# Moving the energies up in TensorE's order and joining four scan products with one wide GpSimd addition

## What is computed

```python
x = whitening(x)         # quaternion batch norm: covariance of 4 channel groups, Cholesky, mix, bias
x = mamba(x)             # layer norm, W_in, causal conv of 4 taps, silu, then the scan:
    def step(hst, xs):
        d_t, B_t, C_t, u_t = xs
        dA = jnp.exp(d_t[:, :, None] * A)
        hst = hst * dA + (d_t * u_t)[:, :, None] * B_t[:, None, :]
        y_t = jnp.einsum('bdn,bn->bd', hst, C_t)      # sum over 16 states
    y = (ys + xc * Dp) * silu(z);  out = W_out y + x
x = self_attention(x)    # softmax(q^T k) over 1024 x 1024 points, gamma * v attention + x
x = nonlocal_block(x)    # softmax of theta^T phi over 1024 x 1024 points, conv, batch norm over all images, + x
```

## Time and profile before

| | |
|---|---|
| median of three runs | 5754.26 us (5746.75 to 5754.81) |
| the profiled execution's own time | 5758.38 us |
| its span | 5756.6 us |
| TensorE, matmul | 4756.3 us busy, 83% |
| VectorE | 5060.5 us busy, 88% |
| ScalarE | 3713.5 us busy, 65% |
| GpSimd | 4706.1 us busy, 82% |
| mean granted TensorE clock | 0.929 of 2.4 GHz |

### The profile page before, as it was taken

One profiled execution on the slowest core, in us unless ns is written; L12 is line 12 of the kernel. 1 busy time (PEld: TensorE's weight loads), 2 busy tenths in 40 slices (PEclk: granted clock), 3 DMA queues, 4 the chain that ended last, 5 costly groups with the idle time before them and its releaser, 6 DMA issues.

```text
span 5756.6 us, 61917 instructions
## 1 busy us (share of the span) xinstructions
PE 4756.3 (83%) x17331; PEld 2758.9 (48%) x17331; DVE 5060.5 (88%) x5978; ACT 3713.5 (65%) x6077; POOL 4706.1 (82%) x3342
## 2 busy tenths in 40 slices
PE   6568888888888888888888888888888888888771
PEld 6134554555445445545554454455455544544451
DVE  4689999999999999999999999999999999999933
ACT  3456666667666666666676667666766766666633
POOL 0698988888888888888888988888888889888910
PEclk9679999999999999999999999999999999999995
DMA  4456555555565555656655655655566566555527
GB/s 130 182 219 223 221 201 218 220 220 211 217 220 211 209 221 216 218 208 220 220 204 219 223 215 211 218 216 204 219 220 220 208 219 225 212 207 219 214 82 295
DMA packets 199099, 1216.87 MB, mean 211 GB/s; under 512 B 27880, under 2 KB 28656, under 8 KB 67696
## 3 DMA queue, kind: packets, MB, share of 16 engines
q1 hardware_dynamic: 194416, 1196.26, 56.6%
q10 hardware_dynamic: 4352, 16.78, 0.7%
HBM read 1158.43 MB, written 54.53 MB: 211 GB/s over the span
## 4 chain that ended last, share of the span: by engine, by line
PE 34%; DVE 29%; issue 14%; ACT 12%; POOL 8%; DMA 1%; DVEq 1%; SPq 0%; POOLq 0%; ACTq 0%
DVE hs L488 12%; PE psE L814 12%; DVE psD L484 11%; PE psA L814 10%; PE psT L814 6%; POOL pa L300 5%; DVE nm L513 3%; PE psT L987 3%; ACT da L680 3%; ACT p L726 3%; PE psY L814 2%; DVE psU L477 1%; POOL pa L306 1%; ACT L649 1%; ACT L751 1%
## 5 line engine op out<-in xcount | busy, mean ns | idle before, releaser
L300 POOL TENSOR_TENSOR pa<-hs,rows_all 128x1024 f32<-128x1024 f32 x1024 | 2411.3, 2355 | 522.7 <-DVE hs L488 522.2
L680 ACT ACTIVATE da<-delta,neg_a 128x512 f32<-128x512 f32 x2048 | 1375.7, 715 | 224.9 <-DVE hs L488 212.6
L484 DVE TENSOR_TENSOR psD<-rows_all,psU 128x512 f32<-128x512 f32 x2048 | 1415.9, 691 | 84.6 <-POOL hlast L304 6.0
L488 DVE TENSOR_TENSOR_SCAN hs<-da,hlast,psD 128x512 f32<-128x512 f32 x1024 | 1310.8, 1280 | 36.3
L306 POOL TENSOR_TENSOR pa<-pa 128x512 f32<-128x512 f32 x1024 | 1301.2, 1271 | 40.1
L488 DVE TENSOR_TENSOR_SCAN hs<-da,psD 128x512 f32<-128x512 f32 x1024 | 1249.2, 1220 | 35.2
L726 ACT ACTIVATE p<-psE,nm 128x1024 f32<-128x1024 f32 x512 | 569.6, 1113 | 633.8 <-DVE nm L513 633.8
L814 PE MATMUL psA<-pt,va 128*128 128x256 f32 x4096 | 954.2, 381 | 1.0 <-DVE x L531 0.6
L814 PEld LDWEIGHTS psA<-pt,va 128*128 128x128 f32 x4096 | 772.5, 192 | 194.9 <-issue 105.9
L513 DVE TENSOR_REDUCE nm<-psE 128x1 f32<-128x1024 f32 x512 | 618.6, 1208 | 275.5 <-PE psE L814 272.3
L690 ACT ACTIVATE pt<-psT 128x512 f32<-128x512 f32 x1024 | 554.9, 591 | 342.5 <-PE psT L987 332.8
(11 more groups left out here) (186 smaller groups left out, 5087.6 us busy)
## 6 DMA issues: line engine op xcount, KB each, us to landing
rows_all<-bc_scratch SPq DMA_DIRECT2D x1024, 1024.0 KB, 4.7
xin<-x SPq DMA_DIRECT2D x40, 512.0 KB, 7.8
xres<-x SPq DMA_DIRECT2D x64, 256.0 KB, 6.3
x_scratch<-x SPq DMA_DIRECT2D x32, 512.0 KB, 4.2
f_scratch<-fa SPq DMA_DIRECT2D x32, 512.0 KB, 6.8
xres<-x SPq DMA_DIRECT2D x8, 512.0 KB, 3.7
x1g<-x SPq DMA_DIRECT2D x8, 512.0 KB, 3.6
fa<-x SPq DMA_DIRECT2D x8, 512.0 KB, 3.7
```

The lines of the kernel that those rows point to most:

```text
L300: pool.tensor_tensor(pa[:, k % PROD, :, :], hs[:, sl, :, :], rows_all[:, slot, 2:4, :], ALU.mult).then_inc(S["prod"], 1)
L484: dve.tensor_tensor(psD[:, :], rows_all[:, slot, j, :], psU[:, :], ALU.mult).then_inc(S["dbu_ok"], 1)
L488: dve.tensor_tensor_scan(hs[:, sl, j, :], da[:, sl, j, :], psD[:, :], hlast[:, h, n_:n_ + 1] if ch else 0.0, ALU.mult, ALU.add).then_inc(S ...
L680: act.activation(da[:, k % 2, j, :], delta[:, h, cols(ch)], ACT.Exp, scale=neg_a[:, h, 2 * q + j:2 * q + j + 1]).then_inc(S["da_ok"], 1)
```

## The change

Two parts. In GpSimd's `products`, the addition of the two states of a pair in every step goes. In odd steps one addition of 1024 columns adds the two pairs as they stand, and one of 512 columns adds the two halves of the result; the semaphore `pair` counts half as many. In TensorE's order the word `energy` moves in some rows, a new word `energy_next` issues the energy of the tile that belongs to the next step, and `add`, `skip0` and `weigh0` move with them.

```diff
@@ -302,12 +302,12 @@
-                    wait(pool, "prod", b, k + 1)
-                    pool.tensor_tensor(pa[:, k % PROD, 0, :], pa[:, k % PROD, 0, :], pa[:, k % PROD, 1, :], ALU.add
-                                       ).then_inc(S["pair"], 1)
                     if k % 2:
-                        wait(pool, "pair", b, k + 1)
-                        pool.tensor_tensor(pa[:, k % PROD, 0, :], pa[:, (k - 1) % PROD, 0, :], pa[:, k % PROD, 0, :], ALU.add
+                        wait(pool, "prod", b, k + 1)
+                        pool.tensor_tensor(pa[:, k % PROD, :, :], pa[:, (k - 1) % PROD, :, :], pa[:, k % PROD, :, :], ALU.add
+                                           ).then_inc(S["pair"], 1)
+                        wait(pool, "pair", b, (k + 1) // 2)
+                        pool.tensor_tensor(pa[:, k % PROD, 0, :], pa[:, k % PROD, 0, :], pa[:, k % PROD, 1, :], ALU.add
                                            ).then_inc(S["quad"], 1)
@@ -1034,22 +1034,22 @@
-                    "centre energy add variance",
-                    "energy turn add weigh0",
+                    "centre add variance",
+                    "add energy turn weigh0",
...
-                    "steps energy add weigh0",
...
+                    "add energy steps weigh0",
...
@@ -1100,6 +1100,8 @@
+                                        if what == "energy_next" and o + 1 in TILE_STEP:
+                                            energy(a, *TILE_STEP[o + 1], scan)
```

More of the change, by code:

```diff
@@ L180, in build @@
             u_ok=2 * NCH, dbu_ok=2 * STEPS, da_ok=2 * STEPS, h_ok=2 * STEPS,
-            hlast_ok=STEPS // 2, prod=STEPS, pair=STEPS, quad=STEPS // 2, quad_mm=STEPS // 2, g_ok=2 * NCH,
+            hlast_ok=STEPS // 2, prod=STEPS, pair=STEPS // 2, quad=STEPS // 2, quad_mm=STEPS // 2, g_ok=2 * NCH,
             x1_mm=NCH, x1_ok=NCH, x1g_ok=NCH,
@@ L1044, in _ @@
                     "energy add",
-                    "energy turn add skip0",
-                    "gates add",
-                    "energy rows turn add",
-                    "steps energy add weigh0",
[L1049 to L1052, removed]
+                    "skip0 energy turn add",
+                    "gates add energy_next",
+                    "rows turn add",
+                    "add energy steps weigh0",
+                    "turn weigh1 turn_more skip1 add energy_next",
+                    "add",
+                    "weigh0 energy turn add",
+                    "turn weigh1 add energy_next",
                 ]
```

## The result

The changed kernel takes 5704.15 us (median of 6 runs, 5701.91 to 5705.79), the kernel before 5754.37 us on the same chip. The ratio is 0.9917, with a 95% interval from 0.9905 to 0.993: 50 us or 0.8% faster. The forecast was 5715 us. In the runs further down, one execution of `tile3_tile4` (6114.69 us) and one of the kernel before (5962.21 us) fell in a slower state of the chip and are left out.

The account below looks back on a forecast made before the run. VectorE's waits, mostly for the energy of tile 3, were taken to bound the kernel. Per image 3.8 - 2.5 - 0.1 = 1.2 us, times 31 = 37 us off 5754, gave a forecast of 5715 us, range 5645 to 5825.

Parts of the forecast that it names:

- What bounds the kernel: VectorE leads at 93% busy inside images; its row maxima wait 6.4 us per image, 5.2 of them at tile 3.
- Energy of tile 3 ahead of `steps`: At tile 3 in both halves, VectorE's waits of 2.48 and 2.70 us shrink to 0.7 each: gain 3.8 us per image.
- the moved `add` fills some of TensorE's idle time: Ahead of tile 3's energy, the add fills some idle time but not most, so 0.7 us of wait stays per half.
- Tile 4 "counted as hidden": At r = 13 tile 4's late energy adds some 1 us of wait, counted as hidden there because GpSimd's chain starts later.
- GpSimd's additions by themselves: In GpSimd's products, 0.19 us less work per pair of steps; nothing gained, since GpSimd is not waited for.
- The chain: GpSimd's gapless work from the product of r = 13 to r = 15's last addition; its quad comes 0.86 us later.
- `add` ahead of the energy of tile 7: At r = 1 the energy stands behind an add waiting for GpSimd's quad: loss 2.5 us per image, bounds 1.2 and 6.6.
- The low clock that I feared there: At tile 7, second half, add and energy both at low clock (2.04 + 3.54 us) would make VectorE wait 3.9 us.
- the wait of 1 to 3 us that I had named as a sign: At tile 7 (r = 1) a new wait of 1 to 3 us appears, TensorE's add released by GpSimd ahead of it.
- the slower rival: New gate at tile 7 wins: 3.1 us more per image, 5850 us, half way 5800; chance 0.32.
- The waits for `rb`: VectorE's waits for rb, 0.93 us in the first half and some 0.3 us later, take up part of tile 7's loss.
- `weigh0` at r = 14: At r = 14 weigh0 ahead of the energy waits for VectorE's attended: loss 0.1 us a half at most, 0.1 in sum.

Follow-up runs that it names:

- tile3_tile4: Kernel before with add and energy ahead of steps at r = 11, plus tile 4's energy right behind the first turn of r = 12: 5679.04 us, ratio 0.9873.
- order_only: Changed kernel's new TensorE order with GpSimd's old additions: 5653.61 us, ratio 0.9824 to the kernel before.
- tile7_free: Changed kernel with the energy of tile 7 ahead of the add again at r = 1: 5671.39 us, ratio 0.9858 to the kernel before.
- tile3_only: Kernel before with one row of the order changed, r = 11: add and energy ahead of steps. 5646.96 us, ratio 0.9816.
- order_skip: New order with GpSimd's old additions, and tile 4's energy moved ahead of skip1 alone: 5643.53 us, ratio 0.9812 to the kernel before.
- tile3_add_behind: Kernel before with r = 11 as energy, add, steps, weigh0, so the add stands behind the energy: 5774.13 us, ratio 1.0043.
- fill_after: Changed kernel with one extra, unneeded matmul ahead of the add at r = 11: 5658.81 us, ratio 0.984 to the kernel before.

## Why the prediction was right, and where it was not

The total, 37 us forecast and 50 measured, came out of terms that were off on both sides, so that its closeness is in good part luck. The forecast was 3.8 - 2.5 - 0.1 = 1.2 us per image. The rows give 2.7 at tile 3, less 1.7 at tile 4 and 0.8 at tiles 6 and 7, plus 1.2 from `rb`, which I had only set against a loss, and 0.4 from VectorE's `xn` (below), for which I had no term: 1.8 us.

- **What bounds the kernel**: right. VectorE's waits for the energy of tile 3 were what could be had, and one row of the order at that place brings 106 us.
- **Energy of tile 3 ahead of `steps`, gain 3.8 us**: the mechanism was right; the size was 2.7 us per image in the changed kernel, inside the bounds of 2.3 and 5.2, and both waits fell below 1.5 us in the mean. The step that failed was "the moved `add` fills some of TensorE's idle time". I did not ask when that `add`'s own quad comes. It is the quad of r = 9, which the GpSimd part makes 1.08 us later by the same arithmetic that I used for r = 15; against the end of tile 2's exponentials it comes 1.1 us later than in order_only. It leaves 2.29 us of idle in one piece, and the clock falls in every image. Without the GpSimd part the row is worth 3.4 us per image (106 / 31).
- **Tile 4 "counted as hidden"**: wrong. It took 1.7 us per image. I expected GpSimd's chain from r = 13 on to swallow that; with GpSimd's old additions 0.86 us less at that place is worth 46 us, 0.75 us a half, so there it is hidden by nothing. In the changed kernel itself this was not tried.
- **GpSimd's additions by themselves: nil**: right (0.9996). The saving per pair of steps is real: 2.357 us for the wide addition against 2 x 1.271. The chain grew by 0.97 us, predicted 0.86.
- **`add` ahead of the energy of tile 7, loss 2.5 us**: the gate is there, and its size was 1.1 us (tile7_free). The low clock that I feared there came in 9 of the 31 second halves (3.0 to 3.6 us), with the wait of 1 to 3 us that I had named as a sign, and else hardly at all (1.88 us), and VectorE was late itself from tile 4, which is what I had named as speaking against the slower rival.
- **The waits for `rb`**: I let them take up 1.2 us of the loss. They went in full, and nearly so in tile3_only, without a gate at tile 7. What ended them was not looked for.
- **`weigh0` at r = 14: 0.1 us**: right, nothing measurable. `skip0` and tile 6 at 0: not tried by themselves.
- **The rivals**: the slower one was half right. GpSimd's quad does take the gain back, to the tune of half of it, but mainly at r = 11, through the clock, and at tile 7 by 1.1 of the 5.4 us that this rival put there. The Trainium skill says that "the default state is throttled, and activity releases the throttle" ("TensorE: Matmul & The Clock Gate", "What's actually happening"). The trace agrees, at the place that I had not looked at: the same energy takes 3.49 us in the changed kernel and 1.98 us with one matmul more in the idle time ahead of it.

## What to carry to other kernels

When an instruction moves up in an in-order queue, everything that moves up with it brings its own wait along: ask for each one when its operand is ready, also where it only looks like filler. A change to an engine that nobody waits for can be free and still cost, once another change makes somebody wait for its result; time the two parts apart and together. On TensorE a short matmul in an idle stretch can pay for itself: here 45 us of 5704. Count over all images at what speed the matmul behind it ran, since one place in the timeline can mislead. And moving an instruction by the smallest step (0.86 us past `skip1`) may win where the larger step moves the wait to the next engine.

## What the runs showed of the hardware

In the changed kernel TensorE stands idle for 2.3 to 2.4 us in one piece ahead of the `add` at r = 11, and all 62 energies of tile 3 take 2.56 to 3.68 us. With one matmul in that time, 61 of 62 take 1.98 us. In how many pieces the idle time comes does not settle it alone. In tile3_only the same two pieces, 1.21 and 1.09 us, stand ahead of a long energy too:

```profile
2503.64 1.10 PE L814 MATMUL psY<-pa,ident 128*128 128x512 f32 x2 [1.21 <-POOL pa L310]
2505.83 3.68 PE L814 MATMUL psE<-ka,qa 128*128 128x512 f32 x4 [1.09 <-ACT p L726]
```

With the idle time split around the `add`, the energy was at 1.98 us in 45 of 62 halves in order_only, 37 in tile3_only, 22 in order_skip and 61 in tile3_tile4. Behind 3.40 us in one piece (tile3_add_behind) it was so in 12. The granted clock from 2506 to 2509 us, inside the long energy, is 0.50, the 1.2 GHz level. What else of TensorE's work before decides it was not tried and stays open.

VectorE's `xn` (L468), its one large operation here with both inputs in SBUF, has no fixed duration. Mean and count over 4000 us, in the kernel before and in the changed one:

```profile
L468 DVE TENSOR_TENSOR xn<-xcen,rstd 128x512 f32<-128x512 f32 x48 | 47.7, 993 | 0.0
```

```profile
L468 DVE TENSOR_TENSOR xn<-xcen,rstd 128x512 f32<-128x512 f32 x49 | 38.3, 781 | 0.0
```

In the kernel with the order alone it runs from 666 to 2535 ns with a median of 1650. Two places of that kernel show why:

```profile
2143.13 0.67 DVE L468 TENSOR_TENSOR xn<-xcen,rstd 128x512 f32<-128x512 f32 x1
2143.17 1.76 POOL L306 TENSOR_TENSOR pa<-pa 128x512 f32<-128x512 f32 x1
...
2223.52 1.27 POOL L306 TENSOR_TENSOR pa<-pa 128x512 f32<-128x512 f32 x1
2223.68 1.67 DVE L468 TENSOR_TENSOR xn<-xcen,rstd 128x512 f32<-128x512 f32 x1
```

The one that starts first keeps its time, and the other is long. Where `xn` starts first, GpSimd's addition takes 1.76 us in place of 1.27. Where the addition starts first, `xn` ends about 0.55 us behind the addition's end. That holds for each of the 43 `xn` of the kernel before, and the 33 of the kernel with the order alone, that took 0.9 us or more. The GPSIMD Engine Reference of the Trainium skill ("Specifications") has the two engines share their SBUF interfaces, with contention for VectorE instructions with two SBUF inputs; these rows agree. The shorter `xn` is 0.4 us of the 1.8 us per image that the change brings, and it moves with every shift between the two engines, so that small differences between such kernels can be this alone. With the extra matmul (fill_after) its mean is 668 ns.
